# Counting the edges of a graph layer in windows of 32 destinations, with the features multiplied by the weights first and aggregated between the counts

## The reference, cut to what matters

```python
def _gcn_conv(x, edge_index, W, b):            # x is already layer-normed
    xw = x @ W.T
    loop = jnp.arange(n)
    row = jnp.concatenate([edge_index[0], loop])
    col = jnp.concatenate([edge_index[1], loop])
    deg = segment_sum(ones_like(row), col, num_segments=n)
    dinv = jnp.where(deg > 0, jax.lax.rsqrt(deg), 0.0)
    msgs = (dinv[row] * dinv[col])[:, None] * xw[row]
    return segment_sum(msgs, col, num_segments=n) + b
...
h = gelu(batch_norm(gcn_conv(layernorm(x))))   # batch_norm over the nodes
x = x + h + layernorm(x)
```

## Time and profile before

| | |
|---|---|
| median of 3 runs | 1264.74 us (1264.42 to 1264.78) |
| span of the profiled execution | 1262.0 us; its own time is not listed beside it, so what lies around the span is taken as 2.7 us from the median |
| busy, of that span | PE 91%, DVE 73%, ACT 41%, POOL 51% |
| counts (first to last matmul of L1580) | 14.9 to 133.8 us |
| aggregation and weights (L1608, L1657) | to 255.6 us |
| first gather of POOL | 284.9 us |

### The profile page before, as it was taken

One profiled execution on the slowest core, in us unless ns is written; L12 is line 12 of the kernel. 1 busy time (PEld: TensorE's weight loads), 2 busy tenths in 40 slices (PEclk: granted clock), 3 DMA queues, 4 the chain that ended last, 5 costly groups with the idle time before them and its releaser, 6 DMA issues.

```text
span 1262.0 us, 15214 instructions
## 1 busy us (share of the span) xinstructions
PE 1145.0 (91%) x3900; PEld 572.9 (45%) x3901; DVE 925.5 (73%) x2783; ACT 514.7 (41%) x1254; POOL 640.5 (51%) x698
## 2 busy tenths in 40 slices
PE   5999999965999998899998998989989889989497
PEld 2555555553444444354444444534444344334243
DVE  6999831357899987978879789788797877665311
ACT  7889103642435343443444434443444333320010
POOL 1000000007667777777777776777767776631322
PEclk9999999986999999999999999999999999989699
DMA  8999000008989999999999999999999999944643
GB/s 336 418 421 418 29 0 1 1 0 345 383 353 388 409 409 408 409 409 410 409 409 408 410 409 408 409 410 408 409 409 397 410 408 381 410 174 163 234 139 109
DMA packets 107763, 406.07 MB, mean 322 GB/s; under 512 B 11946, under 2 KB 12112, under 8 KB 103332
## 3 DMA queue, kind: packets, MB, share of 16 engines
q0 software_dynamic: 92992, 337.10, 67.6%
q1 hardware_dynamic: 14692, 68.07, 13.8%
HBM read 353.24 MB, written 53.00 MB: 322 GB/s over the span
## 4 chain that ended last, share of the span: by engine, by line
PE 53%; DVE 14%; DMA 13%; POOL 9%; issue 5%; ACT 2%; DVEq 2%; ACTq 0%; SPq 0%; POOLq 0%
PE tr L1786 19%; PE acc L1580 8%; DMA big<-in_wdu,idx 7%; PE acc L1608 7%; POOL big L587 6%; PE acc L1714 4%; DMA AT<-in_wdu,idx 4%; DVE big L1313 4%; PE acc L1687 3%; PE tr L1883 3%; PE acc L1657 3%; POOL AT L587 3%; PE tr L1861 2%; PE acc L1698 2%; DVE AT L1313 2%
## 5 line engine op out<-in xcount | busy, mean ns | idle before, releaser
L587 POOL DMA_INDIRECT big<-in_wdu,idx x460 | 434.2, 944 | 435.3 <-DVE idx L1377 279.3
L1786 PE MATMUL tr<-big,diag 128*128 128x512 f32 x920 | 427.1, 602 | 31.8 <-ACT diag L883 31.2
L1313 DVE CUSTOM_DVE_ANT_0 big<-big,acc,prob 128x512 f32<-128x512 f32 x460 | 322.9, 742 | 68.2 <-DMA big<-in_wdu,idx 66.7
L883 ACT ACTIVATE diag<-ident,inner 128x128 f32<-128x128 f32 x576 | 199.3, 393 | 414.2 <-DVE inner L1313 412.3
L1786 PEld LDWEIGHTS tr<-big,diag 128*128 128x128 f32 x920 | 166.9, 190 | 249.0 <-issue 167.1
L587 POOL DMA_INDIRECT AT<-in_wdu,idx x168 | 163.6, 974 | 61.8 <-issue 46.0
L1786 PE MATMUL tr<-AT,diag 128*128 128x512 f32 x336 | 157.0, 600 | 8.7 <-ACT diag L883 8.7
L1313 DVE CUSTOM_DVE_ANT_0 AT<-AT,acc,prob 128x512 f32<-128x512 f32 x168 | 118.0, 743 | 25.2 <-DMA AT<-in_wdu,idx 24.2
L1580 PE MATMUL acc<-outT,diag 128*128 128x512 f16 (+1 forms) x600 | 112.7, 349 | 4.0 <-ACT diag L689 3.8
L996 DVE TENSOR_SCALAR outT<-big 128x1280 f16<-128x1280 f16 x200 | 96.6, 547 | 6.1 <-PE acc L1580 3.2
L1786 PEld LDWEIGHTS tr<-AT,diag 128*128 128x128 f32 x336 | 61.0, 190 | 86.2 <-issue 62.1
(11 more groups left out here) (301 smaller groups left out, 1068.7 us busy)
## 6 DMA issues: line engine op xcount, KB each, us to landing
sorted_rows<-big SPq DMA_DIRECT2D x33, 1280.0 KB, 32.7
big<-in_we SPq DMA_DIRECT2D x8, 1024.0 KB, 14.6
big<-in_wdu,idx POOLq DMA_INDIRECT x460, 10.6
x<-sorted_rows SPq DMA_DIRECT2D x14, 512.5 KB, 3.5
AT<-in_wdu,idx POOLq DMA_INDIRECT x168, 10.8
x<-in_x SPq DMA_DIRECT2D x1, 2304.0 KB
qk<-in_wq SPq DMA_DIRECT2D x1, 2048.0 KB, 15.4
big<-in_w0t SPq DMA_DIRECT2D x1, 1024.0 KB, 12.3
```

Source lines behind the costliest of these rows:

```text
L587: pool.indirect_dma_start(out=k.slot[r * GS + s], out_offset=None, in_=k.wdu_d, in_offset=bass.IndirectOffsetOnAxis(ap=k.idx[i % 2][:, j:j ...
L883: ins = act.activation(k.diag[:, c * P:(c + 1) * P], to, ACT.Relu, scale=k.inner[:, j:j + 1])
L1313: ins = dve.tensor_tensor_reduce(out=row, in0=row, in1=k.Y[i % 2] if i < NT - 1 else k.Yh[j // WIDTH], scale=k.prob[:, (i % 2) * HK + j:(i ...
L1786: ins = pe.matmul(k.O[i % 2], k.diag[:, c:c + P], row, start=(g == 0 and s == 0), stop=(g == groups_of(i) - 1 and s == GS - 1))
```

## The change

The counts are made in 40 windows of 32 destinations (`WIN`, `NW`) in place of 10 tiles of 128.

- A table `table` holds the one-hot of the source within its tile for all 168 + 8 columns of 128 edges; DVE builds it once. A window's chunk is one matmul: the weights are a column of that table, its 128 values 176 elements apart, and the moving operand is a mark of 128 x 320 (source tile and destination within the window) that DVE makes by one instruction.
- A window has `FIXED` = 2 rows of 256 edges in straight code and at least one in a register loop. Each of PE and DVE reads `bnd` at the start of each window (`rows_of`). ACT makes no one-hots.
- In-degrees come before the counts, from a histogram: 168 matmuls of `lo_hot` by `hi_hot` (32 x 40), two more tables of one-hots.
- `x` comes in a second time, transposed (`xT`). POOL subtracts the column mean from the weights, PE multiplies `xT` by them (`weighted`, ten tiles of four 512-column products), and ACT copies with the scale of the source (`keep_xw`). Six of the ten stand between windows.
- The aggregation is 12 parts: four blocks of features by three ranges of 256, 512 and 482 destinations. Eight stand between windows, after the windows named in `PART_AFTER`, four after the last.
- POOL adds the loops, takes them out again and copies `AT` to `few` before it gathers. `wq` and `keys` are loaded only after the last window, behind the zeros in SP's queue, since the table lies in their place. The zeros go out in 68 writes.

```diff
+WIN = 32
+NW = NPAD // WIN
+CODES = NT * WIN
+FIXED = 2
+BLOCK = 44
+TABLE = 4 * BLOCK
+SPANS = [(0, 256), (256, 512), (768, N - 768)]
+PARTS = [(c0, n, o) for c0, n in SPANS for o in range(FT)]
+PART_AFTER = {9: 0, 13: 1, 17: 2, 21: 3, 25: 4, 28: 5, 31: 6, 34: 7}
...
+    sp.wait_ge(k.acc_ready, NW)
     sp.dma_start(k.wq.rearrange("p (f n) -> p f n", n=H * P),
...
+    pool.wait_ge(k.wmean_ready, 1)
+    for f in range(FT):
+        rows = k.w0[:, f * D:(f + 1) * D]
+        pool.tensor_tensor(rows, rows, k.wmean, ALU.subtract)
+    pool.drain().then_inc(k.wc_ready, 1)
...
+    for t in range(NT):
...
+        pool.tensor_tensor(loops(t), loops(t), k.ident[:, :], ALU.subtract)
+        pool.drain()
+        pool.tensor_copy(k.few[:, t * NPAD:(t + 1) * NPAD] if t else k.few0, k.AT[:, t * NPAD:(t + 1) * NPAD])
...
+    def keep_counts(w):
         at = k.AT[:, :].rearrange("p (j c) -> p j c", c=NPAD)
+        act.wait_ge(k.acc_ready, w + 1)
+        act.activation(at[:, :, w * WIN:(w + 1) * WIN], k.banks[w % 2][:, 0:CODES].rearrange("p (j c) -> p j c", c=WIN),
                        copy).then_inc(k.at_done, 1)
+    act.wait_ge(k.coef_ready, 1)
+    kept_after = {0: [1, 2], 1: [3], 2: [4], 3: [5], 4: [6], 5: [7], 6: [8, 9]}
+    keep_xw(0)
+    for w in range(NW):
+        keep_counts(w)
+        for t in kept_after.get(w, []):
+            keep_xw(t)
...
+    def one_hots(out, codes, n, block):
+        cols = slice(block * BLOCK, (block + 1) * BLOCK)
+        return dve.tensor_tensor(out[:, 0:n, cols], codes[:, cols].unsqueeze(1).to_broadcast([P, n, BLOCK]),
+                                 k.iotaX[:, 0:n, :], ALU.is_equal)
...
+    def marks(w, first):
+        end, shift = rows_of(dve, k, w)
+        base = column(dve, k, (first + shift) * 2, 2 * (NS - 1))
+        for row in range(FIXED):
+            if w >= 2 and row == 0:
+                dve.wait_ge(k.fixed_used, w - 1)
+            for c in range(2):
+                ins = dve.tensor_scalar(k.fixed[w % 2][2 * row + c], k.iota,
+                                        k.key[:, 2 * row + c:KEYS][:, bass.ds(base, 1)], -float(CODES * w),
+                                        ALU.subtract, ALU.is_equal)
+            ins.then_inc(k.fixed_ready, 1)
+        with dve.Fori(first, end) as row:
+            col = column(dve, k, (row + shift) * 2, 2 * (NS - 1))
+            dve.wait_ge(k.looped_used, row + 1)
...
+    first = marks(0, 0)
+    dve.wait_ge(k.indeg_psum, 1)
...
+    dve.wait_ge(k.x_in, 48)
     for t in range(NT):
+        stats(k.x[:, t * D:(t + 1) * D], t)
...
+    first = marks(1, first)
...
+    dve.drain().then_inc(k.coef_ready, 1)
...
+    def window(w, first):
+        end, shift = rows_of(pe, k, w)
+        base = column(pe, k, (first + shift) * 2, 2 * (NS - 1))
+        if w >= 2:
+            pe.wait_ge(k.at_done, w - 1)
+        for row in range(FIXED):
+            pe.wait_ge(k.fixed_ready, FIXED * w + row + 1)
+            for c in range(2):
+                ins = chunk(w, base, 2 * row + c, k.fixed[w % 2][2 * row + c], row == 0 and c == 0)
+        ins.then_inc(k.fixed_used, 1)
+        with pe.Fori(first, end) as row:
+            col = column(pe, k, (row + shift) * 2, 2 * (NS - 1))
+            pe.wait_ge(k.looped_ready, row + 1)
...
+    def part(p):
+        c0, n, o = PARTS[p]
...
+        for t in range(NT):
+            ins = pe.matmul(k.banks[2 + p % 4][:, 0:n], k.xw[:, t * D + o * P:t * D + (o + 1) * P],
+                            k.AT[:, t * NPAD + c0:t * NPAD + c0 + n], start=(t == 0), stop=(t == NT - 1))
...
+    weighted(0)
+    pe.wait_ge(k.bounds_ready, 1)
...
+    histogram()
+    weighted(1)
+    weighted(2)
+    in_degrees()
+    weighted(3)
+    pe.wait_ge(k.table_ready, 1)
+    first = 0
+    for w in range(NW):
+        first = window(w, first)
+        if w + 4 < NT:
+            weighted(w + 4)
...
+        if w in PART_AFTER:
+            part(PART_AFTER[w])
+    for p in range(EARLY, len(PARTS)):
+        part(p)
```

More of the change, by code:

```diff
@@ L187, in lay_out @@
+    k.looped = [hots[:, (4 * FIXED + c) * CODES:(4 * FIXED + c + 1) * CODES] for c in range(2)]
     k.wq = k.qk[:, 0:4096]
@@ L219, in lay_out @@
     k.mm = sb("mm", 2, rows=NS)
[L220 to L222 removed]
+    k.lh = sb("lh", 4, rows=NW)
     k.st = sb("st", 6 * NT)
@@ L340, in program @@
         k.x_in = sem("x_in")
+        k.xt_in = [sem(f"xt_in{c}") for c in range(len(CHUNKS))]
         k.w_in = sem("w_in")
@@ L641, in pool_program, with rows_of, column @@
             store(q * XR + r, r)
-def pairs_of(eng, k, t):
-    word = eng.value_load(k.bnd[0:1, t:t + 1], min_val=END, max_val=(NS // 4 * NT + 1) * END - 1)
+def rows_of(eng, k, w):
+    word = eng.value_load(k.bnd[0:1, w:w + 1], min_val=END, max_val=(NS * NW + 1) * END - 1)
     return eng.snap(word >> 12), eng.snap((word & (END - 1)) - SHIFT)
-def column(eng, k, value):
-    return k.nc.s_assert_within(eng.snap(value), 0, KEYS - 2 * BPS,
-                                skip_runtime_bounds_check_because="first <= pair < end, so 2 lo <= col < KEYS - BPS")
+def column(eng, k, value, most):
+    return k.nc.s_assert_within(eng.snap(value), 0, most,
+                                skip_runtime_bounds_check_because="low <= row < NS, the looped row at most FIXED after it")
@@ L656, in act_program, with XW_BANK @@
+def XW_BANK(k, t):
+    return k.banks[(3, 4, 5, 2)[t % 4]]
 def act_program(act, k):
     copy = ACT.Copy
[L658 to L667, removed]
-    ins.then_inc(k.stage_zero, 1)
-    act.wait_ge(k.edgeT_ready, 1)
-    for c, table in enumerate((k.key, k.neg)):
-        ins = act.activation(table[:, 0:2 * NS].rearrange("p (q b) -> p b q", b=2),
-                             k.tr[c][:, 0:2 * NS].rearrange("p (b q) -> p b q", b=2), copy)
@@ new lines, in pe_program, with weighted @@
+    for f in range(FT):
+        ins = pe.matmul(k.banks[2], k.ones, k.w0[:, f * D:(f + 1) * D], start=(f == 0), stop=(f == FT - 1))
+    ins.then_inc(k.wsum_psum, 1)
+    def weighted(t):
+        if t == 0:
+            pe.wait_ge(k.wc_ready, 1)
+            pe.wait_ge(k.pads_made, 1)
+        pe.wait_ge(k.xt_in[t // 4], 16)
+        if t >= 4:
+            pe.wait_ge(k.xw_kept, t - 3)
+        for f in range(FT):
+            ins = pe.matmul(XW_BANK(k, t), k.xT[:, f * NPAD + t * P:f * NPAD + (t + 1) * P], k.w0[:, f * D:(f + 1) * D],
+                            start=(f == 0), stop=(f == FT - 1))
+        ins.then_inc(k.xw_psum, 1)
```

696 lines of the change are left out of this document (325 added, 371 removed).

## The result

The changed kernel takes 1274.6 us (median of four runs, 1273.5 to 1276.5) against 1264.76: ratio 1.008, 95% interval 1.0066 to 1.0094. It is 9.8 us slower where I forecast 9.2 us faster. Its profiled span is 1272.2 us against 1262.0.

The account below looks back on a forecast made before the run. PE's run up to the last product before batch norm, ending at 255.6 us, was taken as the bound. Start, products, parts, windows and clock loss summed to 245.8, the first gather 9.2 us earlier: 1255.5 us, range 1240 to 1262.

Parts of the forecast that it names:

- window period: Windows without cover, between parts: PE's and DVE's sequencers set 2.6 us each, bounds 1.8 and 3.4.
- covered windows: Windows directly behind a product or part, where sequencer and DVE run ahead: about 0.9 us each, 13 of them.
- I take a loss of 2.5 us at two of the eight parts, 5: Parts between windows: PE's lowered clock costs 2.5 us at each of two, 5 us in all.
- the start: From program start through weights, histogram, products and in-degrees: window 0 begins at about 54 us.
- the histogram: Before window 0, PE's 168 matmuls for in-degrees: 0.085 us each, 14.3 us in all.
- the tail: From the last product before batch norm to POOL's first gather: 29.9 us, with POOL's copies hidden.
- The strided rival: PE's reads of values 352 bytes apart are slow in histogram and chunks: 1278 us, or 1332 at fourfold; chance 0.15.
- Second windows: Windows second after a part wait only for the single looped buffer: about 1.0 us each, 8 of them.
- The clock rival: Each of eight parts and the start lose 2.5 us to PE's clock: 20 more, 1275 us; chance 0.10.
- Hand-overs in series: At the windows, each costs 3.4 us and covered ones 2: 36 more, 1291 us; chance 0.10.
- More run-ahead: At the windows, 1.8 us each and no cold part: 14 + 5 less, 1236 us; chance 0.12.
- 18 bare windows: Of windows 1 to 39, the 18 neither behind nor second after a product or part cost 2.6 us each.

Follow-up runs that it names:

- The first experiment: Changed kernel plus one unread f32 product of 512 columns ahead of bare windows from the tenth on; 1266.4 us, ratio 1.0015 to the kernel before.
- the fifth: Changed kernel with each window's rows as program constants, no reads or register loops, histogram weights packed; 1363.0 us beside 1374.4 for the kernel before.
- the sixth experiment: Constants for window rows as well, two whole sets of row buffers, only the histogram's moving values packed; 1344.8 us beside 1374.4 for the kernel before.
- Experiment 7: Changed kernel with the eight parts cut into slices of two to four matmuls behind nearly every window; ratio 0.9876 to the kernel before.
- experiment 9: Changed kernel with sliced parts, histogram one-hots stored packed, DVE's statistics and histogram copy ahead of the table; ratio 0.9766 to the kernel before.

## Why the prediction was wrong

*What held.* DVE's table instructions took 3.09 us each, the fast rate; window period 2.3 to 2.6 us from start to start for 2.6; covered windows 0.8 for 0.9; roots, products, POOL's work behind the last loops, the queries' loads and the out-degree sum as costed. The period held as a sum, not by its terms: I had 0.56 us for PE's reading of `bnd`, and from 150 us on, all 18 reads took 0.30. What fills the rest I did not trace, so some luck is in the 2.6.

*The step that failed* is "I take a loss of 2.5 us at two of the eight parts, 5", together with the start, where I let the products behind the histogram run nearly warm. The first experiment prices the clock between window 0 and the last part at 9.2 us: parts 1 to 3 (4.7), three of the last four (26.77 for 24.53, 2.2) and the windows (2.0). It leaves part 0 at 5.81 us, which takes 4.42 in the fifth, so 1.4 more. The two products behind the histogram add 2.6. That is about 13 us where 5 stood, 8 of the 18.1. I had seen that 36% busy left PE at 0.50, counted the bare gaps, and still put a price at only two of the eight parts. At the start there was no gap to count: the clock fell within the strided histogram, with PE busy throughout.

The clock alone would have left the forecast 1 us faster than the kernel before. The sign turned with the smaller terms: the histogram (2.6), the windows beyond their share of the clock (2.3), the tail (1.4), and the columns themselves, 2.4: at PEclk 1.00 a product took 3.54 us and a part 4.42 or 8.69, where I had 3.41, 4.27 and 8.53. About 1 us more lies in the start and in `weighted(4)`.

*The histogram* was mis-sized less than it was misread: 0.101 us for 0.085, 2.6 us. My comparison was a load of 128 packed weights with one moving column; it hid that a packed histogram takes 0.026 a matmul. The strided rival said "from 0.14 us a matmul it decides", and at 0.101 it did not alone. The chunks, which I thought at risk as well, showed nothing. With 4.3 us for the packed histogram, 10 of the forecast's 14.3 us were a price of the stride that I did not know I was paying.

*Second windows*: 1.0 forecast, 1.4 to 1.5 measured in the six of three rows, 2.7 of the 4.3 us; the two of four rows took 2.8, where 1.75 stood, and the covered windows gave some of it back. The looped row's buffer is freed by the covered window's last chunk only, and mark, signal and matmul follow one another; the sixth experiment, which gives each row a buffer, brings 0.9.

*The tail*: 1.4 us, of it 1.0 in one DVE instruction of one column that took 1.17 us beside POOL's copies, not 0.16. I had costed those copies at nothing.

*The rivals.* The clock rival gave 1275 for a result of 1274.6, but by other places than it named: not 2.5 us at each part, but the first parts, the last four and the start, with the second windows and the histogram beside them. Its number was luck. Hand-overs in series did not set the 3.4 us that this rival named: the period stayed under 2.7 from start to start. By the sixth experiment the shared buffer is worth 11 us once the reads are gone. More run-ahead did not occur.

*What I did not ask* is the most useful finding: whether the parts stand where their cover is worth most. I costed 18 bare windows at 2.6 us and took their number as given. Experiment 7 takes 25 us of that off windows 9 to 39 with an edit of some twenty lines.

Left open: why three strided reads differ so (last section), what fills the window period, and a register loop with a second looped buffer, which was not tried.

## What to carry to other kernels

When two engines' sequencers set a period and the buffers let one run only a window ahead, a long piece of work covers one window, and the next ones stand bare; cut the long piece and put a slice behind each. In this kernel a gap on PE was paid twice, once as idle time and again in the matmuls behind it, so every bare stretch needs a clock term and not only the worst. The strided histogram needed one too, although PE counted as busy in it. And a margin of 9 us on a path of 276 is less than an error of 4% in its terms: sum the plausible error of each before trusting the direction.

## What the runs showed of the hardware

- Values of 2 bytes lying 352 bytes apart: a matmul of 32 weights and 40 moving values takes 0.101 us with both strided, 0.101 with only the moving ones, 0.066 with only the weights, 0.026 with neither. The first is the same at PEclk 1.00 and at 0.50. The clock fell to 0.50 in each of the three histograms with a strided operand, at 100% busy, and stayed at 1.00 in the packed one. Loads of 128 strided weights under 320 moving columns stayed hidden in 0.136 us a chunk, so the cost is not one price per value. The Trainium skill's note on cachelines (page "SBUF — State Buffer") puts a penalty on each access that crosses to a new 16-byte line, which fits the histogram. The Trainium skill lists strided columns as fit for the fast load of 128 weights (page "TensorE: Matmul & The Clock Gate", section "Weight-path perf modes"), which fits the chunks.
- POOL's subtractions of two inputs took from 1.25 to 4.10 us, the longest beside DVE's 3.09 us one-hots; the four together took 6.4 us in one run, 8.5 in another and 10.3 beside the longer one-hots of experiment 9. That the two make each other wait agrees with the Trainium skill, page "SBUF — State Buffer", section "Who interferes with whom". The line of the first experiment (duration ns min/median/max):

```profile
L617 POOL TENSOR_TENSOR big<-big,outT x4: 1254/1623/4103, 17.7 to 22.1; 128x512 f32<-128x512 f32 x4
```

- The same between POOL's copies and DVE's smallest instruction, in the changed kernel:

```profile
L1130 DVE TENSOR_TENSOR bsc<-bsd,par x4: 159/162/1175, 247.9 to 266.1; 128x1 f32<-128x1 f32 x4
```

- One extra product of 512 f32 columns ahead of each bare window from the tenth on held the granted clock at 1.00 (2.4 GHz) from 130 to 165 us, where it had been 0.80.
